# Multi-head attention with one key head: three stack transfers, value products moved ahead of scores, denominators inverted on another engine

## What is computed

```python
q = (x @ wq_w.T + wq_b).reshape(b, t, H, HD)       # b=8, t=512, H=32, HD=32
k = (x @ wk_w.T + wk_b).reshape(b, t, HKV, HD)     # HKV=1
v = (x @ wv_w.T + wv_b).reshape(b, t, HKV, HD)
scores = jnp.einsum('bqhd,bkd->bhqk', q, k1) / jnp.sqrt(jnp.float32(HD))
scores = jnp.where(causal, scores, -jnp.inf)
weights = jax.nn.softmax(scores, axis=-1)
attn = jnp.einsum('bhqk,bkd->bqhd', weights, v1)
return attn @ wo_w.T + wo_b
```

## Time and profile before

| | us |
|---|---|
| median of 3 runs (4253.95 to 4259.86) | 4259.47 |
| the profiled execution's own time | 4256.95 |
| its span, first to last instruction | 4255.2 |
| TensorE busy over the span | 3257.7 (77%) |
| VectorE (DVE) busy | 1840.8 (43%) |
| ScalarE (ACT) busy | 890.0 (21%) |
| GpSimd (POOL) busy | 822.2 (19%) |
| mean granted TensorE clock | 0.857 |

### The profile page before, as it was taken

How to read it: one execution, slowest core, us unless ns; L and a number is a source line. 1 busy time by engine, 2 the same in 40 slices (tenths; PEclk the granted TensorE clock), 3 DMA queues, 4 the chain that set the end, 5 groups by cost and what they waited for, 6 DMA issues and landing times. The chain is left out here.

```text
span 4255.2 us, 42641 instructions
## 1 busy us (share of the span) xinstructions
PE 3257.7 (77%) x16896; PEld 2393.8 (56%) x16896; DVE 1840.8 (43%) x2817; ACT 890.0 (21%) x1620; POOL 822.2 (19%) x1011
## 2 busy tenths in 40 slices
PE   1777878768778778778777677887878878888877
PEld 1545546546446446456455445676766657666655
DVE  3334342342342343342433314555564747464634
ACT  2222121221221221221221201212131312121211
POOL 0011111111111111111111112332232323222311
PEclk9888889889889889889888887898889888888887
DMA  6222122122122221222221131000000010101000
GB/s 198 80 75 67 65 72 82 61 68 80 53 72 85 70 72 65 74 71 72 73 72 55 53 112 52 20 14 27 15 26 24 17 40 1 40 1 40 1 20 20
DMA packets 107306, 234.69 MB, mean 55 GB/s; under 512 B 21178, under 2 KB 40762, under 8 KB 107106
## 3 DMA queue, kind: packets, MB, share of 16 engines
q1 hardware_dynamic: 102592, 228.75, 17.0%
q10 hardware_dynamic: 4514, 3.16, 0.2%
HBM read 139.04 MB, written 41.94 MB: 43 GB/s over the span
## 5 line engine op out<-in xcount | busy, mean ns | idle before, releaser
L400 DVE TENSOR_REDUCE top<-ps_attn 128x1 f32<-128x512 f32 (+3 forms) x704 | 433.2, 638 | 861.2 <-PE ps_attn L546 859.3
L543 PE MATMUL ps_attn<-k_stack,q_stack 96*128 96x512 f32 (+3 forms) x1024 | 347.3, 396 | 458.7 <-DMA q_stack<-q_lo 277.1
L317 ACT ACTIVATE pt<-ps_attn 128x512 f32<-128x512 f32 (+1 forms) x704 | 384.7, 559 | 1174.1 <-PE ps_attn L568 1165.4
L543 PEld LDWEIGHTS ps_attn<-k_stack,q_stack 96*128 96x128 f32 x1024 | 207.2, 219 | 543.8 <-DMA q_stack<-q_lo 297.5
L260 POOL TENSOR_SCALAR_AFFINE_SELECT pt<-pt 128x512 f32<-128x512 f32 x256 | 166.0, 663 | 1726.7 <-ACT pt L317 1726.7
L1225 PE MATMUL ps_mixer<-m_w_hi,m_xt_hi 128*128 128x512 f32 x1024 | 427.5, 417 | 76.6 <-DVE m_xt_lo L1064 76.6
L1226 PE MATMUL ps_mixer<-m_w_hi,m_xt_lo 128*128 128x512 f32 x1024 | 414.3, 405 | 0.0
L1227 PE MATMUL ps_mixer<-m_w_lo,m_xt_hi 128*128 128x512 f32 x1024 | 412.6, 403 | 0.0
L407 DVE RECIPROCAL att<-ps_attn 128x512 f32<-128x512 f32 x64 | 214.9, 3358 | 233.5 <-PE ps_attn L576 233.5
L568 PE MATMUL ps_attn<-q_stack,k_stack 97*128 97x512 f32 (+3 forms) x1024 | 311.4, 366 | 2.3 <-ACT pt L317 1.2
L485 PE MATMUL ps_attn<-xn_hi,wq_hi 128*128 128x512 f32 x512 | 257.9, 504 | 59.3 <-DMA wq_lo<-wq_split 52.5
(11 more groups left out here) (193 smaller groups left out, 5260.3 us busy)
## 6 DMA issues: line engine op xcount, KB each, us to landing
xr<-in_a_x SPq DMA_DIRECT2D x64, 512.0 KB, 3.8
wq_hi<-wq_split SPq DMA_DIRECT2D x64, 512.0 KB, 3.6
wq_lo<-wq_split SPq DMA_DIRECT2D x64, 512.0 KB, 4.5
q_stack<-q_hi SPq DMA_DIRECT2D x512, 64.0 KB, 2.0
q_stack<-q_lo SPq DMA_DIRECT2D x256, 64.0 KB, 2.0
x<-xr SPq DMA_DIRECT2D x32, 512.0 KB, 2.6
m_xs<-x SPq DMA_DIRECT2D x32, 512.0 KB
out<-m_xs SPq DMA_DIRECT2D x32, 512.0 KB
```

What stands on the lines that cost most here:

```text
L317: nc.scalar.activation(pt[k][:, heads[0]:heads[0] + len(heads), :].rearrange("p j t -> p (j t)"), ps[:, ST0 + n % 2, 0:width * len(heads)] ...
L400: nc.vector.tensor_reduce(out, ps[:, S0 + n % 2, 0:width * len(heads)].rearrange("p (j k) -> p j k", k=width), AX.X, ALU.max).then_inc(s_u ...
L543: nc.tensor.matmul(bank[:, m * width:(m + 1) * width], q_stack[0:KROWS, G % 2, j, i * P:(i + 1) * P], k_stack[0:KROWS, b % 2, 0:width], st ...
```

## The change

Four edits are made together.

The columns of wq are permuted during setup, and the rows of bq with them, so that a group's feature rows run over the head first and then over the four heads. One transfer then fills a place of the stack: 3 transfers of 256 KB in place of 12 of 64 KB.

`weigh_rest(M - 1)` stands ahead of the first two score units, and the eight query chunks are spread otherwise over the step.

The reciprocal leaves DVE. ACT copies bank DEN to att (`unload`), POOL raises att to the power -1 (`invert`), DVE multiplies (`divide`).

ACT's `finish_high` and `q_high`, DVE's `divide` and POOL's `inv_sqrt` move to later or earlier places in their lists.

```diff
-    STACK = 3 * GH * DMA
+    STACK = 3 * DMA
...
+        def turned(w, n):
+            return w.rearrange("p (g j d) -> p g d j", j=GH, d=HEAD) if 1 <= n <= CH else w
+
+        def straight(w, n):
+            return w.rearrange("p (g d j) -> p g d j", j=GH, d=HEAD) if 1 <= n <= CH else w
...
-                    nc.scalar.copy(hi, stage(n)).then_inc(staged_hi, 1)
+                    nc.scalar.copy(straight(hi, n), turned(stage(n), n)).then_inc(staged_hi, 1)
...
-                        for j in range(GH):
-                            sp.dma_start(q_stack[place * HEAD:(place + 1) * HEAD, G % 2, j, :].bitcast(F32),
-                                         src[j * HEAD:(j + 1) * HEAD, :].bitcast(F32)).then_inc(qs_in, DMA)
+                        sp.dma_start(q_stack[place * HEAD:(place + 1) * HEAD, G % 2, :, :].bitcast(F32).rearrange("p j t -> p (j t)"),
+                                     src[:, :].bitcast(F32)).then_inc(qs_in, DMA)
...
+                def invert(G):
+                    pool.wait_ge(den_out, G + 1)
+                    nc.gpsimd.tensor_tensor(att[:, :], att[:, :], neg_one[:, :].to_broadcast([P, T]), ALU.pow).then_inc(inv_done, 1)
...
                         for k in range(1, TILES):
                             cut(M - 1, k)
+                        invert(M - 1)
                     if inside(M):
                         cut(M, 0)
...
+                def unload(G):
+                    act.wait_ge(b_done, G + 1)
+                    if G:
+                        act.wait_ge(olo_done, G)
+                    nc.scalar.copy(att[:, :], ps[:, DEN, :]).then_inc(den_out, 1)
...
                 def divide(G):
-                    dve.wait_ge(b_done, G + 1)
-                    if G:
-                        dve.wait_ge(olo_done, G)
-                    nc.vector.reciprocal(att[:, :], ps[:, DEN, :]).then_inc(inv_done, 1)
                     dve.wait_ge(inv_done, G + 1)
                     nc.vector.tensor_tensor(att[:, :], ps[:, AV, :], att[:, :], ALU.mult).then_inc(att_done, 1)
...
-                        tops(M + 1, (0, 1))
-                    if inside(M - 1):
-                        divide(M - 1)
-                    if inside(M + 1):
-                        tops(M + 1, (2, 3))
+                        tops(M + 1, (0, 1, 2))
...
+                        tops(M + 1, (3, 4))
+                    if inside(M + 1):
+                        tops(M + 1, (5,))
+                    if inside(M - 1):
+                        divide(M - 1)
...
-                        q_part(M + 2, (0, 1, 2))
+                        q_part(M + 2, (0,))
                     if inside(M):
                         tops_turned(M)
                     if project:
-                        q_part(M + 2, (3,))
+                        q_part(M + 2, (1, 2))
                     if b is not None:
                         transposes(b, 0)
+                    if inside(M - 1):
+                        weigh_rest(M - 1)
                     if inside(M + 1):
                         scores(M + 1, 0)
                         scores(M + 1, 1)
-                    if inside(M - 1):
-                        weigh_rest(M - 1)
...
-                        if project and u in (1, 3, 4, 5):
-                            q_part(M + 2, ({1: 4, 3: 5, 4: 6, 5: 7}[u],))
+                        if project and u in (0, 1, 2, 4, 6):
+                            q_part(M + 2, ({0: 3, 1: 4, 2: 5, 4: 6, 6: 7}[u],))
```

More of the change, by code:

```diff
@@ L58, in attention_program @@
         var_eps, inv_std, neg_half = sb("var_eps", [P, 2]), sb("inv_std", [P, 2]), sb("neg_half", [P, 1])
+        neg_one = sb("neg_one", [P, 1])
         bo_rows = sb("bo_rows", [P, D])
@@ L99, in _ @@
                 nc.gpsimd.memset(neg_half[:, :], -0.5).then_inc(setup_done, 1)
+                nc.gpsimd.memset(neg_one[:, :], -1.0).then_inc(setup_done, 1)
                 nc.gpsimd.memset(ones[:, :], 1.0).then_inc(setup_done, 1)
@@ L103, in _ @@
                 nc.gpsimd.tensor_tensor(bkv_scaled[:, :], bkv_sb[:, :], kvs_sb[:, :], ALU.mult).then_inc(bkv_ready, 1)
-                pool.wait_ge(setup_done, 3)
+                pool.wait_ge(setup_done, 4)
             @block.scalar
@@ L108, in _ @@
                 params = [(identb_sb[:, :], ident_b), (causal_sb[:, :], causal_b),
-                          (bo_rows[:, :], bo), (bq_sb[:, :], bq), (bkv_sb[:, :], bkv), (kvs_sb[:, :], kv_scale)]
+                          (bo_rows[:, :], bo), (bq_sb[:, :], bq.rearrange("(j d) c -> d j c", j=GH)), (bkv_sb[:, :], bkv), (kvs_sb[:, :], kv_scale)]
                 for dst, src in params:
@@ L125, in _ @@
                     dve.wait_ge(staged_hi, n + 1)
-                    nc.vector.tensor_tensor(lo, stage(n), hi.bitcast(F32), ALU.subtract).then_inc(staged_lo, 1)
-                dve.wait_ge(setup_done, 3)
+                    nc.vector.tensor_tensor(straight(lo, n), turned(stage(n), n), straight(hi.bitcast(F32), n),
+                                            ALU.subtract).then_inc(staged_lo, 1)
+                dve.wait_ge(setup_done, 4)
             @block.tensor
@@ L131, in _ @@
                 pe.wait_ge(mask_done, 2)
-                pe.wait_ge(setup_done, 3)
+                pe.wait_ge(setup_done, 4)
                 pe.wait_ge(shift_done, 1)
@@ L278, in _ @@
                             cut(M - 1, k)
+                        invert(M - 1)
                     if inside(M):
                         cut(M, 0)
+                    if (b := next_row(M)) is not None:
+                        inv_sqrt(b, 2)
                     if inside(M - 1):
                         finish_low(M - 1)
-                    if (b := next_row(M)) is not None:
-                        inv_sqrt(b, 2)
+                    if b is not None:
                         inv_sqrt(b, 3)
@@ L345, in _ @@
                         x_high(b, 0)
+                    if inside(M - 1):
+                        unload(M - 1)
                     if inside(M):
@@ L357, in _ @@
                         x_high(b, 2)
-                    elif inside(M + 2):
+                    if inside(M - 1):
+                        finish_high(M - 1)
+                    if inside(M):
+                        exps(M, (6, 7))
+                    if b is None and inside(M + 2):
                         q_high(M + 2)
                     if inside(M):
-                        exps(M, (6, 7, 8, 9, 10))
+                        exps(M, (8, 9, 10))
                     if b is not None:
@@ L454, in _ @@
                     if inside(M + 1):
-                        tops(M + 1, (4, 5))
+                        tops(M + 1, (3, 4))
+                    if inside(M + 1):
+                        tops(M + 1, (5,))
+                    if inside(M - 1):
+                        divide(M - 1)
                     if b is not None:
@@ L468, in _ @@
                     if inside(M + 1):
-                        tops(M + 1, (9, 10))
+                        tops(M + 1, (8, 9, 10))
                     if b is not None:
```

6 lines of the change are left out of this document (1 added, 5 removed).

## The result

The changed kernel takes 8,936.67 us (median of 4 runs, 8,928.49 to 8,941.13) against 4,256.71 us for the kernel before in the same comparison. The ratio is 2.0992, with a 95% interval of 2.0956 to 2.1028. The forecast was slower, 12,070 us with a likeliest range of 8,500 to 13,000.

The account below looks back on a forecast made before the run. No engine was full; TensorE's stack and score-bank waits set the step. Removing them saved 458 us, but 64 serial powers of 137 us, less 608 us of cover, added 7,811 to 4,257: 12,070 us, likeliest 8,500 to 13,000 (8 in 10: from 3,650).

Parts of the forecast that it names:

- The deciding step: POOL's power of 128x512, priced at 268 ns for each further column: 137 us, with 82 and 145 from other readings.
- The form of the sum: Attention loop: one power in series per step, 64 in all, with copy 0.61 us and product 0.69 us.
- 64 X - 983: Whole change in us, X being the power's time: 64 (X + 1.30) - 608 - 458; +7811 at X = 137.4.
- minus 458.3: TensorE's waits for the query stack's low part (277.1 us) and for a score bank unread by DVE (181.2) both go.
- The cover: Score units beside the power on TensorE, 9.5 us a step, 608 us over 64 steps; they hide powers up to 8.2 us.
- up to 480: TensorE's chain, some 7.5 us at full clock, runs at half of it after each long stop: another 480 us.
- The first rival: POOL's power is not priced by the column; under 8.2 us the whole takes 3,800 us; below about 15 us, chance 0.39.
- The third rival: The stack still comes late: 9 us against 7, losing 96 us of gain; 3,900 us with a hidden power; chance 0.03.
- the 7 us of cover: After the turned scores, TensorE's three query chunks, transpose and late products cover the stack's landing: at least 7 us.
- The fourth rival: DVE's product waits for the power, queuing the seventh reduction; up to 181 us of bank wait returns: 3,980 us; chance 0.02.

Follow-up runs that it names:

- the run with quarters: The changed kernel without copy and power, DVE's reciprocal cut into four 128-column pieces behind the first four reductions, low query part behind unit 9's reduction: 4,132.93 us, ratio 0.9699.

## Why the prediction came right, and where its steps were off

**The deciding step held, its size was too large.** The prediction priced the power by its own rows at one and four columns, not by the subtraction of the same shape. Measured: 81.93 us, where it took 137 and named 82 as one end. The step that was mis-sized is the slope of 268 ns a column, from the mean of L957. The short reading, 1,044 ns, gives 159, and the widths from 1 to 512 bear that out. The 55.5 us too much are 64 x 55.5 = 3,550 us of the forecast. The rest of the sum fell short by some 410, worked out below, which leaves the 12,070 us 3,133 too high. The mechanism came as forecast, the size of its main term did not.

**The form of the sum held.** One power per group in series: halving it took off 64 times the half within 2 us. With the measured power the sum 64 X - 983 gives +4,260, thus 8,517 us where the profiled execution took 8,928.49. It is 411 short, and TensorE's waits and busy times of the two profiles share it out. *Waits:* "minus 458.3" was the step that failed. The two waits went from 458.3 to 209.1, the weights' wait rose by 21.3, and those for a cut, for the shift transfer and for an exponential by 36 together, so some 266 of the 411 were never saved. *The cover:* 64 (X + 1.30) - 608 puts 4,719 us of waiting behind the power; the waits for the product and for the last low part grew by 4,790. The cover was 8.4 us a step instead of 9.5, which is 71 us. *The matmuls:* the same 16,896 kept TensorE busy 69 us longer. I read this as the clock, which went both ways. The first early products behind the 75 us stop take 1.93 us instead of 1.06, at a granted clock of 0.50 in the 5 us from 3103 on. The late products, without a long stop ahead of them, take 2.8 us at 1.00 (3016.61 to 3020.13, less a stop of 0.72) instead of 4.9 at 0.53. I had allowed up to 480 for the first and not seen the second. The last 5 us are small differences.

That the time lay inside the range owes something to luck. Its lower end was the sum at the short reading, 8,520 us, without any of these 411; the range reached up only because the power's price was open.

**The rule that spoke the other way.** The Trainium skill's GPSIMD Engine Reference, section Elementwise, side by side, has 2.6 cycles an element at 1.2 GHz for two inputs. For 512 elements that is an estimate of 1.1 us, and the subtraction is near it at 1,271 ns in the changed kernel. A power of the same shape takes 64 times as long, 160 ns a column, 192 cycles at that clock. The page has no row for a power; for it, the measurement decides.

**The first rival** (a price not set by the column) is refuted by the widths 1 to 64, 256 and 512. Its 3,800 us would not have come even with a short power: 4,016.

**The third rival** had the right suspicion at the wrong price. A 256 KB transfer into 32 partitions does not land after 3.3 us but after 5.6 and 6.8, slower than 512 KB of weights at 4.6. So the third lands 1.24 + 6.8 = 8.0 us after the first issue, against the 7 us of cover, and 50.4 us of stack wait stay, where the rival had 9 us and 96. The three are issued 0.6 us apart, and no run sends one alone, so how much of the landing is one waiting for another is not known. In the kernel before, with nothing else changed, the three transfers shorten TensorE's 48 waits for the stack by 1.1 us each.

**The fourth rival** was half right: the bank wait stays at 158.7 us, though not for the reason given. The stop of 2.51 us before the third unit did go, it is 0.16 us now; another took its place later in the step, where the kernel before had none. DVE's low part of the query waits for ACT, and the last three reductions are queued behind it; the stop of 1.95 us at 3010.41 comes from there. DVE had no such wait for ACT before the change. Its wait in the changed kernel:

```profile
DVE q_lo L435 <- ACT q_hi L338: 332.6, 56, 6.7
```

The same place in DVE's timeline of the kernel with the reciprocal put back, where TensorE goes on at 1112.81:

```profile
1111.40 0.75 DVE L436 SCALAR_TENSOR_TENSOR q_lo<-ps_attn,bq_sb,q_hi 128x512 fp32r<-128x512 f32 x1 [5.52 <-ACT q_hi L337]
1112.07 1.28 DVE L421 TENSOR_REDUCE top<-ps_attn 128x2 f32<-128x512 f32 x2
```

## What to carry to other kernels

Price an operation by rows of the same operation at other sizes, and where a row has two readings, work the slope from each: here the right one stood in the trace as a minimum. A wait struck out of a sum is a gain only up to the next resource's time: put half of the change back and read which wait has taken its place, before believing the total. Before a long instruction is moved to another engine, read its price there; cut into pieces, it can also stay where it is, though here the pieces only repaired a bad place and did not beat the whole one at its old place.

## What the runs showed of the hardware that was not expected

- GpSimd's power costs 0.55 us for one column of 128 partitions and 154 to 159 ns for each further one, up to 81.93 us for 512. Up to 64 columns it was the same for both values (1.5, 300) and both exponents (-1, -0.5). The power of 128x4 in the second half takes some 1,413 ns in 14 of its 16 instances and 1,042 to 1,047 in the last two, before the change and after it, for a reason that no run here shows.
- A 256 KB transfer between SBUF tiles, from 128 partitions into 32, landed 5.6 us (q_hi) and 6.8 us (q_lo) after issue, while one of 512 KB from DRAM landed after 3.7 and 4.6. These figures are not fixed: in the run with quarters the low part landed after 7.8 us and the weights' low part after 5.9.
- DVE's reciprocal of 128x512 from PSUM takes 3.36 us. Cutting it in four costs 0.41 us in all.
